# Negative bit weights by a second queue, gate stores on GpSimd's queue, and the head outputs loaded in pieces, in a recurrent-attention kernel on eight cores

## The reference

```python
xn = layernorm(x)
# attention: 16 heads of 128, blocks of 256 tokens
qkv = silu(xn @ w_qkv.T)
o_inter = (q * q_decay) @ kv
qk = (q @ k.T) * diag_decay;  o_intra = qk @ v
kv = block_decay * kv + (k * k_decay).T @ v
out = norm_w * out * rsqrt(mean(out**2) + 1e-6)      # over all heads
s = (sigmoid(xn @ w_gate.T) * out) @ w_out.T
# bit weights: pweight, nweight are (2048, 2048, 4)
soft = sigmoid(pweight) - sigmoid(nweight)
weight = einsum('oin,n->oi', soft, exps * sigmoid(mask)) * scale
g = silu(xn @ weight.T + bias)
return x + s * g
```

## Time and profile before

| | us |
|---|---|
| median of 2 runs | 2432.28 |
| range of the runs | 2422.57 to 2442.0 |
| the profiled execution, its own time | 2427.02 |
| its span, slowest core (core 1) | 2425.2 |
| spans of the other cores | 2394.1 to 2417.3 |

### The profile page before, as it was taken

How to read it: one execution, slowest core, us unless ns; L and a number is a source line. 1 busy time by engine, 2 the same in 40 slices (tenths; PEclk the granted TensorE clock), 3 DMA queues, 4 the chain that set the end, 5 groups by cost and what they waited for, 6 DMA issues and landing times.

```text
span 2425.2 us, 22646 instructions; the slowest of 8 cores (2394.1 to 2425.2 us)
## 1 busy us (share of the span) xinstructions
PE 1634.8 (67%) x7928; PEld 765.0 (32%) x7928; DVE 868.4 (36%) x1613; ACT 569.5 (23%) x827; POOL 191.1 (8%) x308
## 2 busy tenths in 40 slices
PE   1110544545459999288888888888888887377896
PEld 1110212222124444144343344343443443133342
DVE  5555254445550000223333333333333333623445
ACT  2225355555652212311111111111111111000000
POOL 0002232223320000000000000000000000110000
PEclk9999777767779999699999999999999999588998
DMA  8219899999981112112222201222222200598554
GB/s 191 104 53 121 125 152 157 159 156 164 168 141 40 39 38 57 19 27 44 44 44 44 42 22 24 44 44 44 44 44 44 44 18 9 147 177 175 165 169 148
DMA packets 170512, 211.74 MB, mean 87 GB/s; under 512 B 74016, under 2 KB 114976, under 8 KB 166304
## 3 DMA queue, kind: packets, MB, share of 16 engines
q0 software_dynamic: 135936, 109.07, 34.0%
q1 hardware_dynamic: 34464, 101.23, 12.6%
HBM read 277.37 MB, written 41.94 MB: 132 GB/s over the span
## 4 chain that ended last, share of the span: by engine, by line
PE 46%; DMA 28%; DVE 11%; issue 7%; ACT 5%; SPq 1%; DVEq 0%; POOL 0%; ACTq 0%; POOLq 0%
PE pfA L579 29%; DMA pnbg<-nwT 12%; DMA pnbg<-pwT 6%; DMA xT_fc<-xT 5%; PE pfA L452 5%; PE pS L452 5%; ACT sq_b L724 2%; DVE sT_b L675 2%; DMA wout_sb<-woutT 2%; PE pT L611 2%; DMA outT<-outb 1%; DVE mneg_c L197 1%; PE pS L727 1%; PE pS L663 1%; DMA xtile<-x 1%
## 5 line engine op out<-in xcount | busy, mean ns | idle before, releaser
L579 PE MATMUL pfA<-xnT,wq_sb 128*128 128x512 bf16 x3072 | 723.8, 391 | 46.4 <-ACT q_dim L595 42.6
L579 PEld LDWEIGHTS pfA<-xnT,wq_sb 128*128 128x128 bf16 x3072 | 299.3, 100 | 406.6 <-issue 87.7
L354 PE MATMUL pfA<-xnT,wg_sb 128*128 128x512 bf16 x512 | 145.4, 454 | 302.6 <-ACT gate_stA L364 240.4
L675 DVE TENSOR_TENSOR sT_b<-pS,decT_all 128x512 bf16<-128x512 f32 x128 | 88.4, 691 | 320.4 <-PE pS L663 320.4
L406 DVE TENSOR_TENSOR sgp<-sgp,sgn 128x1024 bf16<-128x1024 bf16 x128 | 88.6, 692 | 264.9 <-ACT sgn L402 264.9
L354 PEld LDWEIGHTS pfA<-xnT,wg_sb 128*128 128x128 bf16 x512 | 56.7, 113 | 391.0 <-issue 352.9
L732 DVE SCALAR_TENSOR_TENSOR O_st<-pO,csb,gate_h 128x256 bf16<-128x256 f32 x128 | 61.9, 484 | 307.9 <-ACT sq_b L724 306.4
L397 ACT ACTIVATE sgp<-pnbg 128x1024 bf16<-128x1024 bf16 x128 | 135.2, 1056 | 144.2 <-DMA pnbg<-pwT 139.0
L896 PE MATMUL pfA<-O_sb,wout_sb 128*128 128x512 bf16 x512 | 126.4, 405 | 55.5 <-DVE s L904 43.5
L402 ACT ACTIVATE sgn<-pnbg 128x1024 bf16<-128x1024 bf16 x128 | 135.1, 1056 | 76.1 <-DMA pnbg<-nwT 70.6
L245 PE MATMUL pT<-id_bf,xntok 128*128 128x128 bf16 x256 | 29.8, 309 | 147.2 <-DVE xntok L234 147.2
(11 more groups left out here) (106 smaller groups left out, 1474.9 us busy)
## 6 DMA issues: line engine op xcount, KB each, us to landing
pnbg<-pwT POOLq DMA_DIRECT2D x128, 256.0 KB, 13.2
pnbg<-nwT POOLq DMA_DIRECT2D x128, 256.0 KB, 12.8
wq_sb<-wqkvT POOLq DMA_DIRECT2D x16, 1536.0 KB, 15.7
xtile<-x SPq DMA_DIRECT2D x16, 1024.0 KB, 5.0
xT_fc<-xT SPq DMA_DIRECT2D x16, 1024.0 KB, 8.0
outT<-outb SPq DMA_DIRECT2D x64, 256.0 KB, 2.8
wg_sb<-wgateT POOLq DMA_DIRECT2D x16, 512.0 KB, 15.5
gate_scr<-gate_stA SPq DMA_DIRECT2D x16, 512.0 KB, 9.5
```

Of the source, the lines that this page charges most:

```text
L354: r = e.matmul(pbank[:], wg_sb[b][:, fc * HD:(fc + 1) * HD], xnT[:, fc * T + tg * 512: fc * T + tg * 512 + 512], start=(fc == 0), stop=(fc ...
L579: r = e.matmul(pfA[par][:], wq_sb[hb][:, fc * 384 + sel * 128: fc * 384 + (sel + 1) * 128], xnT[:, fc * T + tg * 512: fc * T + tg * 512 + ...
L675: tst = sch.op("V", (lambda h, jp: lambda e: e.tensor_tensor(out=sT_b[:, jp * 512:(jp + 1) * 512], in0=pS[jp][:], in1=decT_all[:, h * 512: ...
```

## The change

Five edits.

1. The load of head 0's q, k and v weights moves from the very start of GpSimd's list to the start of the head stage, where it waits for the gate product's end. `wq_sb0` is no longer kept from the start.
2. Negative weights are loaded by SyncE's queue as float32 into three new buffers `pnq`; the wait is for the sigmoid of three units before. Positive ones stay on GpSimd with a cast, in four buffers.
3. The gate store of each head moves from SyncE's to GpSimd's queue, at the same place in the source.
4. The sigmoid of the negative weights reads float32.
5. The load of the heads' outputs in the output stage is cut into four DMAs by token group (2 MB each, rows of 1 KB), and a group of matmuls waits for its own piece.

```diff
-    tok_wq0 = sch.op("G", lambda e: e.dma_start(
-        out=wq_sb0[:].rearrange("p (c j) -> p c j", j=384),
-        in_=wqkvT_ap[0].rearrange("(c p) j -> p c j", p=128)),
-        inc=True, sem="wq0")
...
     pnbg = [esPN.enter_context(nc.sbuf_tensor(f"pnbg{i}", [128, D // 2], BF16))
-            for i in range(8)]
+            for i in range(4)]
+    pnq = [esPN.enter_context(nc.sbuf_tensor(f"pnq{i}", [128, D // 2], F32))
+           for i in range(3)]
...
-            tok_gsd[h] = sch.op("Q", (lambda h, gb: lambda e: e.dma_start(
+            tok_gsd[h] = sch.op("G", (lambda h, gb: lambda e: e.dma_start(
                 out=gate_dram[h], in_=gate_st[gb][:]))(h, gb),
                 waits=[tok_gst[h * NTG + NTG - 1]], inc=True, sem="gsd0")
...
-                    tok_pn[(ui, 1)] = sch.op("G",
+                    tok_pn[(ui, 1)] = sch.op("Q",
                         (lambda ic, n, hf, bq: lambda e: e.dma_start(
-                            out=pnbg[bq][:],
+                            out=pnq[bq][:],
                             in_=nwT_ap[n, ic * 128:(ic + 1) * 128,
                                        hf * HD2:(hf + 1) * HD2]))(ic, n, hf, bq),
-                        waits=[tok_sig.get((ui - 4, 1))],
-                        inc=True, sem=f"pn{bq}")
+                        waits=[tok_sig.get((ui - 3, 1))],
+                        inc=True, sem=f"pq{bq}")
...
-        tok_wq[0] = tok_wq0
+        tok_wq[0] = sch.op("G", lambda e: e.dma_start(
+            out=wq_sb[0][:].rearrange("p (c j) -> p c j", j=384),
+            in_=wqkvT_ap[0].rearrange("(c p) j -> p c j", p=128)),
+            waits=tok_ffn_done + [tok_gsd[NH - 1]], inc=True, sem="wq0")
...
-        tok_oload = sch.op("Q", lambda e: e.dma_start(
-            out=O_sb[:].rearrange("p (c t) -> p c t", t=T),
-            in_=o_dram.rearrange("c p t -> p c t")),
-            waits=tok_c_done + [tjoin, tsjoin], inc=True, sem="olo")
+        tok_oload = {}
+        for tg in range(NTG):
+            tok_oload[tg] = sch.op("Q", (lambda tg: lambda e: e.dma_start(
+                out=O_sb[:].rearrange("p (c t) -> p c t", t=T)[
+                    :, :, tg * 512:(tg + 1) * 512],
+                in_=o_dram[:, :, tg * 512:(tg + 1) * 512].rearrange(
+                    "c p t -> p c t")))(tg),
+                waits=(tok_c_done + [tjoin, tsjoin]) if tg == 0 else [],
+                inc=True, sem=f"olo{tg}")
...
-                    waits=[tok_wout[fc], tok_oload, tok_ev3.get((gidx - 4, "s"))], inc=True)
+                    waits=[tok_wout[fc], tok_oload[tg],
+                           tok_ev3.get((gidx - 4, "s"))], inc=True)
```

More of the change, by code:

```diff
@@ L163, in build_program @@
     xnT = esABC.enter_context(nc.sbuf_tensor("xnT", [128, NFC * T], BF16))
-    wq_sb0 = esABC.enter_context(nc.sbuf_tensor("wq_sb0", [128, NFC * 384], BF16))
     esPN = contextlib.ExitStack()
     pnbg = [esPN.enter_context(nc.sbuf_tensor(f"pnbg{i}", [128, D // 2], BF16))
-            for i in range(8)]
+            for i in range(4)]
+    pnq = [esPN.enter_context(nc.sbuf_tensor(f"pnq{i}", [128, D // 2], F32))
+           for i in range(3)]
     sgp = [esPN.enter_context(nc.sbuf_tensor(f"sgp{i}", [128, D // 2], BF16))
@@ L379, in emit_pn_chunk @@
                     bg = ui % 4
-                    bq = 4 + ui % 4
+                    bq = ui % 3
                     sp = ui % 2
@@ L402, in emit_pn_chunk @@
                         (lambda ui, bq, sp: lambda e: e.activation(
-                            out=sgn[sp][:], in_=pnbg[bq][:], func=AF.Sigmoid))(ui, bq, sp),
+                            out=sgn[sp][:], in_=pnq[bq][:], func=AF.Sigmoid))(ui, bq, sp),
                         waits=[tok_pn[(ui, 1)], tok_comb.get((ui - 2, 0))], inc=True)
@@ L486, in sbC @@
             return esC.enter_context(nc.sbuf_tensor(name, list(shape), dtype))
-        wq_sb = [wq_sb0, sbC("wq_sb1", (128, NFC * 384), BF16)]
+        wq_sb = [sbC(f"wq_sb{i}", (128, NFC * 384), BF16) for i in range(2)]
         gate_h = [sbC(f"gate_h{i}", (128, T), BF16) for i in range(2)]
```

## The result

The changed kernel is slower. Its median is 2501.6 us over 11 runs (2482.8 to 2699.5), that of the kernel before 2425.0 over 10 (2422.6 to 2442.0), and the ratio is 1.025, with a 95% interval of 1.022 to 1.028. The profiled execution took 2489.3 us, with a slowest core of 2487.5.

What follows compares the result with a forecast made beforehand. The 16 transfer engines were taken to bound the weight stage. From the profiled 2427.0 us, +74 for the gate store, +1 for fewer buffers, 0 for the head stage and +3 for the output stage gave 2505 us, range 2462 to 2550.

Steps and rivals of the forecast that it cites:

- +74 for the steps: Weight stage: 13 steps between gate groups grow from 32.7 to 38.4 us through the gate store on GpSimd.
- chunk-2 step: Weight stage: the step before chunk 2, already without lead at 40.3 us, was to stay as it was.
- (a): Weight-stage step: wait from gates' end to first data, 13.2 us plus 1.9 for the store, so 15.1 us.
- rival B: Weight stage: not slower, if the first positive load lands within 10.35 us after the gates; 2416 us, chance 0.04.
- (b): Weight-stage step: eight pairs of positive and negative sigmoids on ScalarE, taken as 21.2 us.
- A: Weight stage: lead lost but transfers catch up, steps of 35.5 to 36.3 us; 2473 us, chance 0.15.
- Negative weights through SyncE: worth 0: Weight stage: float32 negatives on SyncE's queue leave a step's transfer work and ScalarE's rate unchanged, so 0 us.
- The start of the stage, +1 us: Start of the weight stage: three buffers instead of four cost one load of lead, 1.6 us, taken as 1.
- The head stage, 0: Head stage: loading the first head's weights there costs 0, hidden by ScalarE's decay tables; without these 15.7 us.
- The output stage, +3: Output stage: four pieces start TensorE earlier but delay g and xT; between -11 and +14 us, taken as +3.
- D: Weight stage: the order on GpSimd does not bind, so only small terms remain; 2431 us, chance 0.02.
- C: Weight stage: dearer steps of 42.3 us, with core 1's own wait and 22.5 us for pairs; 2555 us, chance 0.17.

Runs made afterwards that it cites:

- five-buffer kernel: The changed kernel with the gate store issued late and five instead of three float32 buffers for negative weights; 2459.8 us, ratio 1.011.
- third set: Four kernels on one chip: before again 2429.5 us, changed again 2484.8, changed with float32 negatives by GpSimd 2434.0, changed with all weights float32 by SyncE 2406.9.

## Why the prediction was right or wrong

**The mechanism.** Right for the store, and incomplete: the step got longer for a second reason that the prediction had put at nothing (below). The store's issue stands right behind the last gate sigmoid, gate weights and positives right behind the store, and one long wait a step is the result. With no load of the bit weights behind it, the store costs nothing. Alone, in the kernel before, it gives a step of 38.6; that this is close to the 38.4 of the sum is chance, since the sum was made for the changed kernel, with negatives ready, and there the step is 36.5. The forecast of 2505 is 16 us above the profiled execution, and the surplus is in its largest term: +74 for the steps, measured +52.5 for the 13 and -4.8 for the chunk-2 step, which the prediction left as it was. That the total came out so near is partly luck: an overestimate of 26 us in the steps met some 10 us too little in the other terms. (The lower end of the range, 2462 us, goes by its own sum with a step of 35.1 and not 35.3.)

**(a), the wait of 15.1 us.** Measured 13.1, in its mean over cores and steps. It is the 13.2 of the cold step of the kernel before without the 1.9 added for the store. The gate weights behind the gates landed 13.3 us after issue in that cold step of core 1 and 9.6 us (median, 300 to 700 us) in the changed kernel, as the condition of rival B had it (quicker because negatives are in place), so they may have given back what the store took; the parts were not measured singly.

**(b), the pairs: 21.2 us.** Measured 36.5 - 13.1 - 2.05 = 21.4, right for a wrong reason. The prediction read 2.54 us a pair in the earlier trace rows as ScalarE's own pitch. With both inputs there it is 1.90 us ((426.07 - 420.37) / 3 in the timeline above, where one more pair lies between the last two), so eight pairs need 15.2. The rows used for the 2.54 carry waits of 0.29 and 0.37 us themselves; they showed the pace of the loads. Most of the rest is the new wait for negatives, 67 us in 49 waits, about 5 us a step. So the argument that ScalarE's 22.4 us exclude a shorter step (against rivals A and B) did not hold.

**"Negative weights through SyncE: worth 0."** This is the step that failed. Of the 4.0 to 4.2 us by which a step became longer, about 1.8 to 2.0 belong to it (34.4 with nothing held and five buffers, against 32.3 to 32.6 on that chip) and the other 2.0 to 2.4 to the store. The equality of a packet's cost, 192 and 204 ns, was no proof: what each queue costs alone is equal (32.3 and 32.4), and what both cost side by side isn't. The Trainium skill, "DMA: Bandwidth & Descriptors", section "Issuing engines are not separate DMA queues", says that issuing from several engines saves only the time of the issuing. The runs agree that the second issuer won nothing (34.4 against 32.3 to 32.6); of the loss that section says nothing.

Inside it the cause is not fully shown. One reading is turn-taking: the earlier trace rows show the two queues moving the same number of packets, 1357 and 1356, and so do the rows of the five-buffer kernel, 291 and 291, so that behind 256-byte packets of gate weights each turn of GpSimd's queue waits for a 4 KB packet of SyncE's. The gate weights' 24.9 us to landing instead of 16.0, and positive loads that come late behind them, fit it; so does the wait that shrank by 3.7 us when the gate weights were moved out of the way. The other reading is that packets of two queues overlap less well (share 1.03 against 1.09). Against it stand the kernel with all weights by SyncE, which has gate weights in the second queue nearly all the time and runs at 32.4 us with a share of 1.02, and the work itself: share times step is 1.09 x 32.6 = 35.5 and 1.03 x 34.4 = 35.4, so the lower share goes with the longer step and gives no cause for it. The five-buffer kernel with its gate weights out of the way would separate them, and was not run.

Had the two simply added up, the waiting store at its own price of about 6 us and the split at 1.8 to 2.0 on top of 32.5, the step would be 40 us. It is 36.5, so the two prices don't add: in the changed kernel the negatives can be issued while GpSimd waits, which is the likely reason and was not tested apart.

**The start of the stage, +1 us.** Measured +5.3. The term counted the lost buffer, and that was the wrong thing: with five buffers head 0's gates still end at 259.4 us, against 252.4 and 252.8 in the two kernels with the old weight stage on that chip, while with float32 negatives by GpSimd they end at 253.5, against 253.3. So the start, too, is longer only where the weights are on two queues. The same 253.5 shows that the moved load of head 0's weights won nothing there, as the prediction had it.

**The head stage, 0.** Right: +1.3 with the gate product before it, and the second wait shrank as the first start moved. The load was hidden by the tables.

**The output stage, +3.** Right in kind: an earlier start of TensorE (6.5 us of the at most 11.2), given back by g and xT behind the pieces. These were forecast 22 us later (2157 against 2135), and the first tile came 10.2 us later. The pair profiled has +7.4, the mean over all kernels +2.9 and the third set 0, so the size is not settled.

**The rivals.** D fell: the order binds. B fell: the wait was 13.1, over its 10.35. C, steps of 42.3 us, was seen on no core of any run. A was nearer in the step (35.5 to 36.3, against 36.5 measured and 38.4 forecast), and as far off in the time (2473 us, 16 below the profiled execution), but it was not as told: the engines did not catch up to a bound of work plus idle stretch, with a share of 0.94 to 0.96 left, below the 1 that was its sign; two effects of another size than assumed ended near it. The forecast share was 0.9.

## What to carry to other kernels

Read each DMA queue as a list in order: before a store that waits for late compute is moved to another queue, look at which loads stand behind it there and who needs them next; two loads issued ahead of the stores won 42 us in the output stage, more than any other edit here. A stream of loads split over two issuers was not free here although its packets cost the same, so measure the split by itself. A pitch that is read as an engine's floor should come from rows with no wait between them.

## What the runs showed of the hardware that was not expected

- The same weight loads took 32.3 us a step when all were issued by GpSimd and 32.4 when all came from SyncE, but 34.1 to 34.9 when divided, positives to one and negatives to the other, at a transfer share of 0.93 to 1.05 over their cores.
- A load of gate weights (512 KB, in 256-byte packets, by GpSimd) landed 16.0 us after issue with the bit weights in the same queue, 24.9 with half of them in SyncE's (five buffers), 39.6 with all of them there, and 9.6 where SyncE's queue was idle beside them.
- Writing float32 in place of bfloat16 on chip did not slow the loads: 228 against 157 GB/s moved, at 32.3 and 32.6 us a step.
- A ScalarE pair of sigmoids of 1024 columns each has a pitch of 1.90 us with its data in place, less than twice the listed 1.04 to 1.06 us of one: the listed durations overlap.
- In the three sets, each on another chip, the same kernel before took 2437.3, 2429.1 and 2429.8 us, so 8 us between two sets say nothing of a kernel.
